# Two attention stages on one core: another opening order in the first; in the second, split first stores, channels-outermost loads and a GpSimd select in place of added masks

## The reference, cut to what matters

```python
x = x + attn_a(layernorm(x))     # 4 batches, 16 heads x 16, causal convolution, running sum
x = x + ffn(layernorm(x))
x = x + attn_b(layernorm(x))     # causal softmax attention, 16 heads x 8
x = x + ffn(layernorm(x))
```

```python
# attn_a
xc = conv4(x) + conv_b                                # 4 taps along time, each channel alone
q = qk / max(|qk|, 1e-12), with qk = xc @ qk_w.T       # per head, k = q
g = sigmoid(xc @ g_w.T + g_b)
state = (v * cos(t * freqs) + v * shift(k)) * g,  v = xc @ v_w.T
decay = gamma ** t
out = (cumsum(state * decay) / (decay + 1e-6)) * q    # then @ o_w.T and a layer norm
# attn_b
Q, K, V = heads(x @ Wq.T), heads(x @ Wk.T), heads(x @ Wv.T);  Q, K = rope(Q), rope(K)
probs = softmax(where(causal, Q @ K.T / sqrt(8), -inf))
out = (probs @ V) @ Wo.T
```

## Time and profile before

| | us |
|---|---|
| time, median of 3 runs | 2264.09 (2260.16 to 2266.58) |
| the profiled execution | 2268.87, its span 2267.1 |
| PE busy | 2085.4 (92% of the span) |
| DVE busy | 1793.4 (79%) |
| ACT busy | 1390.3 (61%) |
| POOL busy | 1166.4 (51%) |
| attn_a, 0 to 172.7 | PE 113.5, DVE 131.7, ACT 105.2, POOL 21.8 busy |
| attn_b, 900.7 to 1524.6 | its opening to about 994, steady groups 1090 to 1493, the last group after that |

### The profile page before, as it was taken

One profiled execution on the slowest core, in us unless ns is written; L12 is line 12 of the kernel. 1 busy time (PEld: TensorE's weight loads), 2 busy tenths in 40 slices (PEclk: granted clock), 3 DMA queues, 4 the chain that ended last, 5 costly groups with the idle time before them and its releaser, 6 DMA issues. The chain is left out here.

```text
span 2267.1 us, 45147 instructions
## 1 busy us (share of the span) xinstructions
PE 2085.4 (92%) x16918; PEld 1082.1 (48%) x16918; DVE 1793.4 (79%) x2386; ACT 1390.3 (61%) x3475; POOL 1166.4 (51%) x529
## 2 busy tenths in 40 slices
PE   5687899999999997799999999987899999999997
PEld 2233555555555553343333333324555555555554
DVE  6886889989899993566777777716888999899993
ACT  7555576666666664346565656665666666666753
POOL 0117778777777771135000000016877777777770
PEclk9899999999999999889999999999999999999999
DMA  2004111112111111212111111113112111111111
GB/s 61 0 1 125 32 36 43 38 34 48 34 37 45 34 34 37 93 46 72 66 50 50 41 44 52 32 29 108 34 37 45 34 43 39 34 44 42 34 34 42
DMA packets 85564, 101.16 MB, mean 45 GB/s; under 512 B 13305, under 2 KB 59329, under 8 KB 83045
## 3 DMA queue, kind: packets, MB, share of 16 engines
q1 hardware_dynamic: 82917, 96.58, 16.1%
q10 hardware_dynamic: 2432, 1.70, 0.3%
HBM read 35.98 MB, written 8.39 MB: 20 GB/s over the span
## 5 line engine op out<-in xcount | busy, mean ns | idle before, releaser
L831 POOL TENSOR_TENSOR ffn_RN<-ffn_SS,ffn_mhalf 128x16 f32<-128x16 f32 x128 | 372.5, 2910 | 282.2 <-DVE ffn_SS L777 281.7
L1930 DVE TENSOR_REDUCE attn_b_NX<-attn_b_s 128x1 f32<-128x512 f32 (+3 forms) x608 | 385.4, 660 | 144.9 <-PE attn_b_s L1632 140.5
L825 POOL TENSOR_TENSOR ffn_QK<-ffn_T 128x1024 f32<-128x1024 f32 x128 | 421.4, 3293 | 19.4 <-DVE ffn_T L725 19.2
L576 ACT ACTIVATE ffn_PB<-ffn_s,ffn_NM 128x128 f32<-128x128 f32 x1024 | 359.9, 385 | 102.2 <-DVE ffn_NM L747 102.2
L1841 ACT ACTIVATE attn_b_PT<-attn_b_s 128x1024 f32<-128x1024 f32 (+3 forms) x352 | 298.3, 870 | 200.5 <-PE attn_b_s L1663 196.0
L612 ACT ACTIVATE ffn_SQ<-ffn_w 128x1024 f32<-128x1024 f32 x128 | 131.0, 1024 | 312.4 <-DVE ffn_T L725 312.1
L819 POOL TENSOR_TENSOR ffn_PB<-ffn_PB,ffn_RDEN 128x1024 f32<-128x1024 f32 x128 | 243.6, 1903 | 23.6 <-DVE ffn_RDEN L710 23.6
L367 PE MATMUL ffn_w<-ffn_Wqkv,ffn_H 128*128 128x512 f32 x512 | 245.2, 602 | 9.9 <-ACT ffn_SQ L612 5.6
L576 ACT ACTIVATION_READ_ACCUMULATOR ffn_PB<-ffn_s,ffn_NM 128x1 f32 x1024 | 230.9, 226 | 0.0
L1632 PE MATMUL attn_b_s<-attn_b_KS,attn_b_QS 72*128 72x512 bf16 (+3 forms) x768 | 220.2, 335 | 4.8 <-DVE attn_b_NX L1930 1.4
L741 DVE TENSOR_TENSOR ffn_QK<-ffn_QK,ffn_RN 128x1024 f32<-128x1024 f32 x128 | 221.5, 1730 | 0.4 <-POOL ffn_RN L831 0.3
(11 more groups left out here) (256 smaller groups left out, 3760.9 us busy)
## 6 DMA issues: line engine op xcount, KB each, us to landing
ffn_Voff<-ffn_Vcur SPq DMA_DIRECT2D x248, 128.0 KB, 2.3
attn_b_QS<-attn_b_qk_parts SPq DMA_DIRECT2D x48, 192.0 KB
attn_b_KS<-attn_b_qk_parts SPq DMA_DIRECT2D x48, 192.0 KB
ffn_H<-ffn_Y SPq DMA_DIRECT2D x64, 128.0 KB, 2.5
ffn_H<-ffn_U SPq DMA_DIRECT2D x64, 128.0 KB, 2.5
attn_b_qk_parts<-attn_b_RP SPq DMA_DIRECT2D x8, 768.0 KB, 10.2
ffn_rope<-in_ffn_rope_dram SPq DMA_DIRECT2D x4, 1024.0 KB, 8.0
attn_b_rope<-attn_b_OS SPq DMA_DIRECT2D x252, 16.0 KB
```

The lines of the kernel that those rows point to most:

```text
L576: last = act.activation(PB[:, x % 2, e, p, :], s_ps[:, e, p * P:(p + 1) * P], ACT.Exp, bias=NM[:, x % 2, e, p:p + 1], accum_out=DEN[:, x % ...
L825: pool.tensor_tensor(QK[:, x % 2, :, :, :].rearrange("p c q k -> p (c q k)"), T1[:, :, :, :].rearrange("p c h k -> p (c h k)"), T2[:, :, : ...
L831: pool.tensor_tensor(RN[:, x % 2, :], SS[:, x % 2, :], mhalf[:, :], ALU.pow).then_inc(rnorm, 1)
L1930: dve.tensor_reduce(NX[:, m % 2, c, g:g + pack, i], s1_ps[k % 2][:, 0:pack * (hi - lo)].rearrange("p (q w) -> p q w", q=pack), AX_X, ALU.m ...
```

## The change

In attn_a nothing is added or removed; orders change. **DVE** leaves `angles(1)` until all 8 chunks are normed and both first convolutions are done, and does `decays(0)` ahead of `convolve(2)`. **ACT** makes the reciprocal decay right after the second copy of `X` (k = 1 of its loop) and does `sigmoid(0)` and `square(0)` ahead of copying the turned `Wo`. **PE** does `gate(0)` and `query(0)` before it waits for the last two chunks and turns `Wo`, and `gate(1)` ahead of the fold; `query(0)` waits for six chunks and not for eight.

In attn_b **SP** stores the first 32 channels of b = 0 alone (`store_first_rows`, semaphore `s_first_rows`), issues `load(0)` behind them, and then the other 96 channels; every load reads with channels as the outermost of its axes (8, 3, 4096) where it was the parts (3, 8, 4096), and the rows in SBUF follow that order. ACT's `first_part(1, w)` also waits for the first rows' store. From group 3 on (SELECTS = 3) **PE** adds no mask in `exp_unit`; **POOL** sets the part above the diagonal of `PT` to zero by an `affine_select` of 128 x 4 x 128 float32 per slot (`select_future`, semaphore `s_masked`), and PE's `value_block` waits for it. POOL's queue keeps its order up to `values(4)`, which comes earlier by one group.

```diff
...
                     else:
-                        pe.wait_ge(n_out, NCH)
+                        pe.wait_ge(n_out, NCH - 2)
...
             pe.wait_ge(s_w, 16 * N_W)
+            gate(0)
+            query(0)
...
             last.then_inc(wo_turned, 1)
-            gate(0)
-            query(0)
+            gate(1)
...
             last.then_inc(wo_mm, 1)
-            gate(1)
...
                     act.activation(X[:, half(k)], e_ps[:, k % 2, :], ACT.Copy).then_inc(xe, 1)
+                if k == 1:
+                    act.wait_ge(s_tab, TABLES)
+                    act.activation(rdecay[:, :, :], decay[:, :, :], ACT.Ln, bias=tiny[:, :]).then_inc(s_rln, 1)
+                    act.wait_ge(s_rln, 1)
+                    act.activation(rdecay[:, :, :], rdecay[:, :, :], ACT.Exp, scale=-1.0).then_inc(s_rexp, 1)
...
                     first_tap((k - 5) // 2)
-            act.wait_ge(s_tab, TABLES)
-            act.activation(rdecay[:, :, :], decay[:, :, :], ACT.Ln, bias=tiny[:, :]).then_inc(s_rln, 1)
-            act.wait_ge(s_rln, 1)
-            act.activation(rdecay[:, :, :], rdecay[:, :, :], ACT.Exp, scale=-1.0).then_inc(s_rexp, 1)
+            sigmoid(0)
+            square(0)
...
                .then_inc(wo_copied, 1)
-            sigmoid(0)
-            square(0)
...
             angles(0)
-            for b in range(NB):
-                norm_out(2 * b)
-                norm_out(2 * b + 1)
-                if b == 1:
-                    angles(1)
-                    dve.wait_ge(s_w, 16 * N_W)
-                if b:
-                    convolve(b - 1)
+            for k in range(4):
+                norm_out(k)
+            dve.wait_ge(s_w, 16 * N_W)
+            convolve(0)
+            for k in range(4, 6):
+                norm_out(k)
+            convolve(1)
+            for k in range(6, 8):
+                norm_out(k)
+            angles(1)
             decays(0)
+            convolve(2)
...
         s_parts_out = [sem("q_out"), sem("k_out")]
+        s_first_rows = sem("first_rows")
+        FIRST_ROWS = BG * BD
...
         o_read = [sem("o_read0"), sem("o_read1")]
-        s_lden, s_rden, s_scaled = sem("lden"), sem("rden"), sem("scaled")
+        s_lden, s_rden, s_scaled, s_masked = sem("lden"), sem("rden"), sem("scaled"), sem("masked")
+        SELECTS = 3
...
                 sp.wait_ge(p3, 2 * b + w + 1)
-                sp.dma_start(qk_dram[w][:, b * P:(b + 1) * P, :].rearrange("a c t -> c a t"), RP[:, w, :, :])\
+                lo = 0 if b else FIRST_ROWS
+                sp.dma_start(qk_dram[w][:, b * P + lo:(b + 1) * P, :].rearrange("a c t -> c a t"), RP[lo:P, w, :, :])\
...
+
+            def store_first_rows(w):
+                sp.wait_ge(p3, w + 1)
+                sp.dma_start(qk_dram[w][:, 0:FIRST_ROWS, :].rearrange("a c t -> c a t"), RP[0:FIRST_ROWS, w, :, :])\
+                  .then_inc(s_first_rows, 16)
...
                 rows = slice(m * BG * BD, (m + 1) * BG * BD)
-                sp.wait_ge(s_parts_out[0], 16 * (m // 4 + 1))
+                if m:
+                    sp.wait_ge(s_parts_out[0], 16 * (m // 4 + 1))
+                else:
+                    sp.wait_ge(s_first_rows, 16 * 2)
...
                     at = slice(a * PARTS * BD, (a + 1) * PARTS * BD)
-                    q = qk_dram[0][a, rows, :].rearrange("(e g) t -> e (g t)", g=BG).unsqueeze(0)\
-                        .broadcast_to([PARTS, BD, BG * T])
+                    q = qk_dram[0][a, rows, :].rearrange("(e g) t -> e (g t)", g=BG).unsqueeze(1)\
+                        .broadcast_to([BD, PARTS, BG * T])
                     sp.dma_start(QS[at, m % RING, :, :].rearrange("p g t -> p (g t)"), q).then_inc(s_load[m % RING], 16)
-                sp.wait_ge(s_parts_out[1], 16 * (m // 4 + 1))
+                if m:
+                    sp.wait_ge(s_parts_out[1], 16 * (m // 4 + 1))
...
                     at = slice(a * PARTS * BD, (a + 1) * PARTS * BD)
-                    k = qk_dram[1][:, rows, :].rearrange("c (e g) t -> c e (g t)", g=BG)
+                    k = qk_dram[1][:, rows, :].rearrange("c (e g) t -> e c (g t)", g=BG)
...
             for w in range(2):
+                store_first_rows(w)
+            load(0)
+            for w in range(2):
                 store_parts(0, w)
-            for m in range(RING):
+            for m in range(1, RING):
...
                 each = max(1, 512 // pitch)
-                for q in range(0, pack, each):
+                selected = n >= SELECTS
+                for q in range(0, 0 if selected else pack, each):
...
                                          KS[:, n % RING, g + q, j * P:(j + 1) * P],
-                                         QS[:, n % RING, g + q, j * P + lo:j * P + hi], start=lo > 0, stop=True,
+                                         QS[:, n % RING, g + q, j * P + lo:j * P + hi],
+                                         start=(q * pitch + lo) % 512 == 0 if selected else lo > 0, stop=True,
...
                 pe.wait_ge(probs, last_exp(n, j) + 1)
+                if n >= SELECTS:
+                    pe.wait_ge(s_masked, NT * (n - SELECTS) + j + 1)
...
                 wait(act, s_parts_out[w], 16 * b)
+                if b == 1:
+                    act.wait_ge(s_first_rows, 16 * 2)
...
             values(0)
-            for m in range(NG):
-                offsets(m)
-                if m == 0:
-                    values(1)
-                    turn_and_add(2, 1)
-                elif m == 1:
-                    parts_of(2)
-                    for w in range(2):
-                        turn_and_add(3, w)
-                    values(2)
-                else:
-                    if m == 2:
-                        parts_of(3)
-                    if m + 1 < NG:
-                        values(m + 1)
+            def select_future(n, j):
+                pool.wait_ge(probs, last_exp(n, j) + 1)
+                at = PT[:, j % 2, :, 0:P]
+                pool.affine_select(at, at, [[0, BG], [1, P]], ALU.is_ge, 0.0, base=0, channel_multiplier=-1)\
+                    .then_inc(s_masked, 1)
+
+            offsets(0)
+            values(1)
+            turn_and_add(2, 1)
+            offsets(1)
+            parts_of(2)
+            for w in range(2):
+                turn_and_add(3, w)
+            values(2)
+            offsets(2)
+            parts_of(3)
+            values(3)
+            offsets(3)
+            values(4)
+            for n in range(SELECTS, NG):
+                for j in range(NT):
+                    select_future(n, j)
+                    if j == MAX_SPLIT - 1 and n + 1 < NG:
+                        offsets(n + 1)
+                if n + 2 < NG:
+                    values(n + 2)
...

```

## The result

The changed kernel takes **2247.0 us** (median of 5 runs, 2244.0 to 2249.5); the kernel before took 2266.6 us beside it (2260.2 to 2270.2). The ratio is 0.9906, its 95% interval 0.9893 to 0.9919: about 21 us faster. The forecast was 2245, range 2234 to 2268. A second set of five rounds gave 0.9907 (0.9892 to 0.9922).

A forecast was written before the change was run, and what follows sets the result against it. It took PE to bound the steady steps, though not alone, and chains of waits the two attn openings. 4.5 + 9 + 8.4 - 1 - 2 = 18.9 us off the profiled 2268.9 gave 2250.0, or 2245 at the median; range 2234 to 2268.

The forecast's parts named there:

- attn_b's opening: Start of attn_b: eight DMA engines instead of three hide the first group's load, the norm is last; 9 us saved.
- last group: Last group of attn_b: no maxima fill PE and a select stands in the last chain; 1 us lost.
- new instruction: POOL in attn_b: an instruction of unknown kind ahead of the first select, hidden by nothing; 2 us lost.
- attn_a's opening: Start of attn_a: the reordered work brings `Q` to 59.9 with DVE last instead of ACT; 4.5 us saved.
- masks off PE, a step: Steady steps of attn_b from group 3: dropping PE's masks, 1.8 us a step, gains 1.3 us a step.
- the new wait, a step: Steady steps of attn_b: value blocks wait 1.17 us for POOL behind the last exponential; unhidden stalls cost 0.6 us a step.
- D: Time of one POOL select in attn_b, which had no row of its own; taken as 0.95 us.
- steps together: Steady steps of attn_b, groups 3 to 14: net 0.7 us a step in 12 steps, 8.4 us saved.
- the 8.6 us: Opening of attn_b: PE's first scores start at 938.3, when the norm is ready, instead of 946.88.
- Perhaps 1.5 more: Opening of attn_b: possible further gain, since the first 16 value matmuls took 3.55 us at half clock, the next 2.02.
- The slow-select rival: attn_b: slow selects stall PE at every block, whole change eaten at about 1.6 us a select; 2274 to 2314; chance 0.15.
- The rival by which the masks come back as waits: Steady steps of attn_b: PE waits for DVE instead, masks give only 0.6, eaten by stalls; time 2254; chance 0.15.

The follow-up runs named there:

- a_only: Kernel before with only the new opening order of attn_a; ratio to before 0.9978 (0.9959 to 0.9997).
- selects_only: Kernel before with only POOL's selects in place of PE's masks from group 3 on; ratio to before 0.9959 (0.9944 to 0.9975).
- mask_and_select: Changed kernel with PE's masks kept beside the selects; a step of 32.24 us, ratio to before 0.9965 (0.9951 to 0.9980).
- select_twice: Changed kernel with each select done twice; a step of 32.53 us, ratio to before 0.9991 (0.9978 to 1.0003).
- after_again: The changed kernel itself, unchanged, run again in the third set; median 2249.2 us, ratio to before 0.9907 (0.9892 to 0.9922).
- conv_first: Changed kernel with attn_a's third convolution ahead of the decays on DVE; median 2247.1 us, ratio to before 0.9902 (0.9887 to 0.9916).

## Why the prediction was right

The sum was 18.9 us; the stretches give 19 to 22, and the ratio 21. The mechanisms were the forecast ones in all three places: DVE last in attn_a, eight engines and the norm last in attn_b, masks off PE at the price of a wait for POOL. The sizes were less good. In the table, cover is the time by which a value block comes later than its last exponential in any case, and which hides the wait. The total was nearer than its terms, and that is luck: attn_b's opening and the last group came out 4 us worse than forecast, the steps, the new instruction and attn_a 4.3 us better.

| term | predicted | measured | step that was off |
|---|---|---|---|
| attn_a's opening | 4.5 | 5.0 (a further 2.6 in the tail, in 4 of 6 profiles with this order) | none; `Q` at 59.9 forecast, 59.46 found |
| attn_b's opening | 9 | 6.9 | the wait to be saved was that of one late execution; the clock's part did not come |
| masks off PE, a step | 1.3 | 0.88 | how much DVE takes back |
| the new wait, a step | -0.6 | 0 | D = 0.95 for 0.64, cover 0.65 for 0.88 |
| steps together | 8.4 | 10.2 | the two above, one against the other |
| last group | -1 | -2.9 | no row was worked through |
| new instruction | -2 | 0 | bound taken from rows of real work |

- **attn_a.** The steps on DVE came as described, the collision included: 6.01 us for the convolution, forecast at 5.9. ACT's first norm result was 2.4 us earlier than forecast, which changes nothing, since DVE is last.
- **attn_b's opening.** The engines' number (8), what is late next (the norm) and the 8.6 us (8.5 found) came as forecast against before. But the 8.6 us hold 1.6 that no change had to win: the first load of before went out 2 us later behind its stores than in any other profile, old opening or new. Against `a_only` and `selects_only` it is 6.9 us at the first score as at the first offsets. "Perhaps 1.5 more" did not come either: both sets of value matmuls run at the half clock, as they do with the old opening in `a_only` and `selects_only`. And the 5.5 us that the forecast took for the whole store, with its hope for a quarter of it, came from the same late load: it is 3.5 for either.
- **The masks.** I counted half of a mask's time in the slots in which PE waits for a maximum, and all of it in others. It was too much: `mask_and_select` measures 32.24 - 31.36 = 0.88 us, half of the 1.8 that the masks take on PE.
- **The wait.** Its form was right: 0.07 + D + 0.14 behind the last exponential, and slots 6 and 0 with the least cover. D was too high: 0.64 lies between the fill's 0.525 and the doubled copy's 0.79, and not above both. But D alone doesn't make the stall zero: with the cover of 0.65 that the prediction gave slot 6, 0.2 us would be left. `select_twice` gives the covers: a wait of 1.55 us less stalls of 0.67 and 0.41 is 0.88 and 1.14, so slot 6 kept its cover when the masks went.
- **The last group.** There the blocks have less cover, and some have none: POOL is waited for seven times, 3.5 us, half of it in two blocks (0.80 and 0.91).
- **The new instruction** ahead of the first select shows no time: the copy ends at 1090.09 and the first select starts at 1090.19, the same 0.10 us as in every later group.

```profile
1089.69 0.40 POOL L2053 COPY attn_b_VQ<-attn_b_VB 128x256 f32<-128x256 f32 x1 [12.33 <-PE attn_b_o L1702]
1090.19 0.64 POOL L2080 TENSOR_SCALAR_AFFINE_SELECT attn_b_PT<-attn_b_PT 128x512 f32<-128x512 f32 x1
...
1121.05 0.40 POOL L2053 COPY attn_b_VQ<-attn_b_VB 128x256 f32<-128x256 f32 x1 [3.63 <-PE attn_b_o L1702]
1121.55 0.64 POOL L2080 TENSOR_SCALAR_AFFINE_SELECT attn_b_PT<-attn_b_PT 128x512 f32<-128x512 f32 x1
```

- **The slow-select rival** was the right thing to fear: the whole change turns at about twice the D that was found. The rival by which the masks come back as waits (0.6 left of 1.8) was half true.
- One sentence ahead of the diff is wrong: POOL's `values(4)` stands where it stood in the queue, with nothing earlier by a group.

## What to carry to other kernels

When work goes from a full engine to an idle one, find the wait that it adds and subtract, slot by slot, the time that already lies between producer and consumer: here 0.85 us of cover met 0.85 us of wait, and doubling the price took nearly the gain of the whole change. Where a step has no other work to fill with (the last group), keep the old way. A DMA share that is a round number of sixteenths, and equal to an axis of the transfer, is a finding by itself: that change of axes was worth 7 us, and the reordering around it nothing. And before a wait is counted as a gain, it is well to see a second execution of the same kernel: here 1.6 of 8.5 us were one execution's own.

## What I had not expected of the hardware

**The clock.** The half level falls at places that a change moves about, for the same work. Tail of attn_a, PE in the kernel before, in the changed kernel, and in its second run (`after_again`), each after 4.5 us of idle time:

```profile
154.71 3.75 PE L1011 MATMUL attn_a_e<-attn_a_OUT,attn_a_Woc 128*128 128x512 f32 x4 [4.49 <-DVE attn_a_gained L1277]
...
161.01 3.27 PE L1011 MATMUL attn_a_qk<-attn_a_OUT,attn_a_Woc 128*128 128x512 f32 x4
```

```profile
150.33 3.44 PE L1011 MATMUL attn_a_e<-attn_a_OUT,attn_a_Woc 128*128 128x512 f32 x4 [4.47 <-DVE attn_a_gained L1278]
...
155.42 1.88 PE L1011 MATMUL attn_a_qk<-attn_a_OUT,attn_a_Woc 128*128 128x512 f32 x4
```

```profile
148.72 3.75 PE L1011 MATMUL attn_a_e<-attn_a_OUT,attn_a_Woc 128*128 128x512 f32 x4 [4.47 <-DVE attn_a_gained L1278]
...
155.03 3.29 PE L1011 MATMUL attn_a_qk<-attn_a_OUT,attn_a_Woc 128*128 128x512 f32 x4
```

The matmuls after the idle time run slow in all three (four in 3.4 to 3.8 us), but the group after them, 3.27 us in before, takes 1.88 in the changed kernel and 3.29 in its second run. It is worth 2.6 us, with the same program. The short form stands in four of the six profiles with the new order (and in both with the convolution moved), and in none of the five with the old one; what decides is not shown. In the second ffn stage, 40-us windows behind its start (columns as above) show the same, before and after:

```profile
1524.63:1564.63 40.00, 29.99 (x117) 14.71 (x118) 22.07 (x31) 18.60 (x39) 30.14 (x16) 0.85 0.37 107
1564.63:1604.63 40.00, 32.25 (x320) 18.80 (x318) 29.42 (x35) 22.99 (x72) 29.79 (x14) 0.93 0.27 79
```

```profile
1503.51:1543.51 40.00, 28.55 (x154) 13.63 (x154) 23.76 (x33) 20.04 (x42) 31.55 (x17) 0.96 0.37 107
1543.51:1583.51 40.00, 32.15 (x300) 19.62 (x300) 30.24 (x35) 23.67 (x81) 30.84 (x13) 0.96 0.30 85
```

The granted clock is 0.85 and 0.93 in the one, 0.96 and 0.96 in the other, and the stage took 3.7 us less; in the second run it took 742.3 us, as before. Nothing in the change touches it. So of the 24.8 us between the two spans, 3.7 are chance, and 2.6 more hang on where the half clock falls in attn_a's tail.

**The engines' rate.** Three engines moved 79 GB/s, 26 each; eight moved 170, 21 each, where the forecast had 26 each and 211.

**POOL beside DVE.** POOL's product takes 3.3 us beside three of DVE's convolution operations, which together go from 3.92 to 6.01 us; beside the first operation of `A`, that one goes from 1.23 to 2.06. Taken one by one, it is a single operation that pays: in the changed kernel the product ends at 55.82 and the first of the three operations takes 3.37 us, to 56.90; the other two take 1.28 each. In `conv_first` the product ends at 59.75 and the first operation of `A` at 60.83. Both end 1.08 us behind the product, and the operations of `Q`, which run beside it there, are no longer than otherwise (0.68). The order on DVE chooses which operation pays, and about 1 us of it can be won.
